# Two self-attentions of a decoder: second scores nine heads behind, weighted products a quarter later, turned maxima in the last quarter of a step

## The reference, cut to what matters

```python
att = jnp.einsum('bhqd,bhkd->bhqk', q, k) * (1.0 / np.sqrt(HD))
att = jnp.where(causal[None, None], att, -jnp.inf)   # the first only
att = jax.nn.softmax(att, axis=-1)
y = jnp.einsum('bhqk,bhkd->bhqd', att, v)
```

## Time and profile before

| what | us |
|---|---|
| median of 3 runs (lowest, highest) | 941.11 (940.72, 942.71) |
| the profiled execution | 941.59 |
| its span, first to last instruction | 939.7 |
| PE busy | 847.7 (90% of the span) |
| DVE busy | 561.1 (60%) |
| ACT busy | 480.4 (51%) |
| POOL busy | 256.1 (27%) |

### The profile page before, as it was taken

How to read it: one execution, slowest core, us unless ns; L and a number is a source line. 1 busy time by engine, 2 the same in 40 slices (tenths; PEclk the granted TensorE clock), 3 DMA queues, 4 the chain that set the end, 5 groups by cost and what they waited for, 6 DMA issues and landing times.

```text
span 939.7 us, 19518 instructions
## 1 busy us (share of the span) xinstructions
PE 847.7 (90%) x6498; PEld 695.7 (74%) x6498; DVE 561.1 (60%) x1561; ACT 480.4 (51%) x1154; POOL 256.1 (27%) x541
## 2 busy tenths in 40 slices
PE   5999879999999999999999968885897888887788
PEld 3888668888888888888888756663796566665565
DVE  3876466555655566655655347774544577666474
ACT  2455465555555555555555315664464476677141
POOL 3864120000000000000000047551075577776110
PEclk9999999999999999999999989999899899999995
DMA  7000000000000000000000030001222000000000
GB/s 270 2 2 1 1 1 1 1 1 1 0 0 0 0 0 0 0 0 0 0 0 0 1 115 1 2 1 28 88 47 59 1 1 0 0 0 0 24 1 22
DMA packets 9410, 15.85 MB, mean 17 GB/s; under 512 B 816, under 2 KB 5040, under 8 KB 8976
## 3 DMA queue, kind: packets, MB, share of 16 engines
q1 hardware_dynamic: 8400, 13.23, 4.2%
q0 software_dynamic: 960, 1.97, 0.9%
HBM read 13.16 MB, written 2.03 MB: 16 GB/s over the span
## 4 chain that ended last, share of the span: by engine, by line
PE 76%; ACT 7%; DVE 6%; issue 6%; POOL 3%; DMA 1%; ACTq 1%; DVEq 0%; POOLq 0%; SPq 0%
PE psum L875 9%; PE psum L887 9%; PE psum L855 5%; PE psum L856 5%; PE psum L857 5%; PE psum L847 5%; PE psum L598 4%; ACT arena L1301 4%; PE psum L840 3%; PE psum L617 3%; PE psum L635 3%; PE psum L956 2%; PE psum L566 1%; PE psum L1034 1%; PE psum L648 1%
## 5 line engine op out<-in xcount | busy, mean ns | idle before, releaser
L1818 DVE TENSOR_REDUCE xnegmax<-psum 128x1 f32<-128x768 f32 x128 | 122.4, 956 | 139.5 <-PE psum L857 139.3
L1405 ACT ACTIVATE arena<-psum,xnegmax 128x768 f32<-128x768 f32 x128 | 115.5, 903 | 139.5 <-DVE xnegmax L1818 97.8
L2265 POOL COPY acur<-A_all 128x128 f32 (+1 forms) x18 | 5.2, 293 | 388.1 <-PE psum L840 388.1
L875 PE MATMUL psum<-pack_a,arena 128*128 128x128 f32 x768 | 106.8, 275 | 0.2 <-ACT arena L1396 0.2
L1249 ACT ACTIVATE arena<-psum 128x384 f32<-128x384 f32 (+1 forms) x128 | 69.5, 546 | 71.2 <-PE psum L620 42.1
L855 PE MATMUL psum<-kv_high,xq_high 128*128 128x384 f32 x256 | 101.5, 396 | 1.8 <-DVE kv_low L1813 1.6
L875 PEld LDWEIGHTS psum<-pack_a,arena 128*128 128x128 f32 x768 | 87.5, 141 | 13.9 <-issue 12.3
L1396 ACT ACTIVATE arena<-psum 128x512 f32<-128x512 f32 x128 | 75.9, 593 | 42.5 <-PE psum L875 42.5
L887 PE MATMUL psum<-arena,xv 128*64 128x256 f32 x768 | 89.9, 383 | 0.0
L856 PE MATMUL psum<-kv_low,xq_high 128*128 128x384 f32 x256 | 86.8, 339 | 0.0
L857 PE MATMUL psum<-kv_high,xq_low 128*128 128x384 f32 x256 | 86.7, 339 | 0.0
(11 more groups left out here) (309 smaller groups left out, 1853.6 us busy)
## 6 DMA issues: line engine op xcount, KB each, us to landing
w1all<-in_w SPq DMA_DIRECT2D x1, 2048.0 KB, 8.2
arena<-in_w SPq DMA_DIRECT2D x1, 2048.0 KB, 10.8
pack_v<-in_pack_v SPq DMA_DIRECT2D x1, 1088.0 KB, 9.0
pack_l<-in_pack_l SPq DMA_DIRECT2D x1, 1079.5 KB, 12.0
pack_q<-in_pack_q SPq DMA_DIRECT2D x1, 1024.0 KB, 6.9
pack_a<-in_pack_a SPq DMA_DIRECT2D x1, 653.0 KB, 6.1
pack_f<-in_pack_f SPq DMA_DIRECT2D x1, 556.0 KB, 9.9
x<-in_x SPq DMA_DIRECT2D x2, 256.0 KB, 3.0
```

The lines of the kernel that those rows point to most:

```text
L875: last = transpose(bank[4 + (3 * u + c) % 2][:, (2 * i + h) * P:(2 * i + h + 1) * P], xprob[:, u % 2, h * KEYS + kt * P:h * KEYS + (kt + 1 ...
L1405: activation(xprob[:, u % 2, half * KEYS:(half + 1) * KEYS].rearrange("p (c w) -> p c w", c=2), src, ACT.Exp, bias=xnegmax[:, u % 2, half: ...
L1818: v.tensor_reduce(xnegmax[:, u % 2, half:half + 1], banks_pair(half), AX.XY, ALU.max, negate=True)\
```

## The change

One constant and a few conditions of the three order loops change. Nothing is computed that was not computed before.

```diff
-LAG = 8
+LAG = 9
@@ PE
-                        if j == 0 and 0 <= it - 3 < H:
+                        if j == 1 and 0 <= it - 3 < H:
                             weighted(it - 3)
-                        if j == 1 and it >= 7 and (it - 7) % G == 0:
+                        if j == 2 and it >= 7 and (it - 7) % G == 0:
                             result_turned((it - 7) // G)
-                        if j == 2 and 0 <= it - 1 < H:
+                        if j == 3 and 0 <= it - 1 < H:
                             maxima_turned(it - 1)
-                        if j == 2 and 0 <= it - 3 < H:
+                        if j == 3 and 0 <= it - 3 < H:
...
                             back_to_tokens(it - 3)
@@ ACT
-                        if j == 1 and 0 <= it - 3 < H:
+                        if j == 2 and 0 <= it - 3 < H:
                             empty_weighted(it - 3)
-                        if j == 1 and it >= 7 and (it - 7) % G == 0:
+                        if j == 2 and it >= 7 and (it - 7) % G == 0:
                             result_ready((it - 7) // G)
@@ DVE
-                for it in range(H + 3):
+                for it in range(H + 4):
...
-                        if j == 2 and 0 <= it - 1 < H:
-                            shifted_queries(it - 1)
-                        if j == 3 and 0 <= it - 3 < H:
-                            divided(it - 3)
+                        if j == 0 and 0 <= it - 2 < H:
+                            shifted_queries(it - 2)
+                        if j == 0 and 0 <= it - 4 < H:
+                            divided(it - 4)
                     aside(it)
```

## The result

The changed kernel takes 966.25 us (median of 4 runs, 965.66 to 967.72) where the kernel before takes 941.63 in the same runs: a ratio of 1.0263 [1.0245, 1.0281]. It is slower by 24.6 us. The forecast was slower by 18.2; the time lies 0.25 us above the upper end of the range. The profiled execution took 966.82 us with a span of 965.0, against 941.59 and 939.7.

A forecast was written before the change was run, and what follows sets the result against it. Both loops were taken to run at the pace of PE's stream. Att1's intervals 10.0, att0's 4.8 and norm work 3.4 sum to 18.2 us, giving 959.3 from the median of 941.11; range 951 to 966.

The forecast's parts named there:

- Head and end: First and last steps of each attention: one first scores more ahead, one less at the end; 0, within 1 us each.
- The interval in att1: Turned maxima to weighted products in att1: each interval 0.77 us longer, waiting for shifted queries; 13 intervals, 10.0 us.
- rival 3: More idle time on PE lowers the granted clock for 2 us in each of 13 att1 steps: 972 us, chance 0.03.
- rival 1: In att1 the new wait takes the place of the turned maxima's old 0.53 wait: 952.4 us, chance 0.08.
- rival 2: POOL's split holds att1's turned maxima; the extra quarter frees them, saving up to 7.1 us: 934.0, chance 0.03.
- rival 4: No difference: the turned maxima's wait goes and the new wait takes back as much: 941 us, chance 0.02.
- ACT's copy of slots: It also waits for the shifted queries, but PE reads its keys only in the next step: taken at nothing.
- the weights are not pulled ahead: At the shifted queries' reader, the load starts after the wait; pulled ahead, it would save 3.9 us, giving 955.4.
- the 2.75: Summed length in us of att1's new interval from turned maxima to weighted products, against 1.98 before.
- att0's intervals: Turned maxima to weighted products in att0: 3.08 against 2.71 us, 0.37 longer in 13 intervals, 4.8 us.
- the norm work: DVE work ending att0 steps 2, 4, 6, 8 delays the next maxima by 0.96 or 0.74, two each: 3.4 us.

The follow-up runs named there:

- the sixth experiment: Kernel before, with turned maxima and back to tokens moved past three score pairs and shifted queries directly behind, weighted products unmoved: 935.05 us, ratio 0.9893.
- the fifth experiment: Kernel before, with only the shifted queries on DVE moved a quarter later, behind one further head's maxima: 955.4 us, ratio 1.0126.
- the first experiment: Changed kernel, with the shifted queries put directly behind the step's last maxima on DVE, ahead of norm work and next maxima: 945.64 us, ratio 1.0008 to before.
- third experiment: Changed kernel, with norm work of att0 steps 2, 4, 6, 8 put behind the shifted queries and two maxima: 964.61 us, ratio 1.0214 to before.

## Why the prediction came out below the time

The mechanism was forecast rightly; the sum was too small, 18.2 us for 24.6. Three of its steps failed. Head and end, put at 0, measured 1.8 us. The interval in att1, put at 0.77, measured 0.85 to 0.93, which is 1.4 us in all. And the clock, for which the sum had no term because rival 3 was put away, fell behind the longest wait of att0, 1.35 us. Without any one of the three the time would have come out inside the range, whose end it passed by 0.25.

**Right: the mechanism and its place.** In every full interval of att1 L617 waits for L1620, W to M is as long as before (2.73 against 2.72) and L648 still waits 0.53. With that rivals 1, 2 and 4 are out: the new wait ate nothing of the old one, and M does not go earlier. The changed kernel gave POOL's split of the maxima the extra quarter of rival 2, and the wait stayed; the sixth experiment put a third score pair between W and M, and it went. So the copy sets M. The term put at nothing, ACT's copy of slots, was rightly so: in att1 L1240 waits for Q 13 times, 7.1 us, but PE stands still for keys only once, 0.4.

**Right: the weights are not pulled ahead.** The load of the reader's weights in the step above:

```profile
622.10 0.31 PEld L598 LDWEIGHTS psum<-kz,slots 128*128 128x128 f32 x2
623.25 0.30 PEld L617 LDWEIGHTS psum<-qs,kz 128*128 128x128 f32 x2 [0.84 <-DVE qs L1620]
```

It starts 0.05 after Q's end (622.79 + 0.41 = 623.20) and not during the 0.84 us in which the loader was idle. The Trainium skill, page "TensorE: Matmul & The Clock Gate", section "Step-by-step: what each phase is for", has loads pulled ahead of matmuls in flight. For this load the row decides against it. The weights here are the keys of a head, which the first scores have read nine heads earlier; the late queries are the other operand. So it is the wait ahead of the load that held it.

**Mis-sized: the interval in att1, 0.77.** Of the thirteen intervals, forecast at 10.0 us, twelve grew by 0.85 to 0.93 and the last by 0.62, 11.4 together. Two terms of the 2.75 were too short. The slots took 621.74 - 621.19 = 0.55 and not 0.48; from the reader to W it was 623.69 - 623.26 = 0.43 and not 0.33. Both prices came from rows with other neighbours ahead. From the reader to W it is 0.43 behind a wait, of 0.64 here and of 0.17 in the fifth experiment, and 0.33 in the sixth without one. The slots are not a matter of the wait: they take 0.56 behind back to tokens in the sixth experiment too (609.47 to 610.03), where M does not wait. The sum left out the slow start of the row behind M, 0.09 in the old order, which now falls on the slots.

**Right in size: att0's intervals and the norm work.** The plain intervals grew by 0.38 (forecast 0.37), 5.0 in 13. The norm work gave 3.6 beyond that (forecast 3.4), though not evenly: the first step 1.76 in all instead of 1.33, half of it since DVE came to the moments 0.20 later than thought and half since this interval was 2.46 and not 2.71 before; the others 1.01, 1.30 and 1.01 for 1.11, 1.33 and 1.11.

**Wrong: "head and end, I take 0".** In att0 the first scores come 0.43 earlier against the first M (in the first experiment too, so this is M's place), and the first M to the second takes 4.49 instead of 3.67 (3.68 in the first experiment, so this too is Q's place); with -0.2 at the end that is +1.0. In att1 the way to the second M gives 0.5 and the last two intervals -0.23 + 0.53 = 0.3. Head and end are 1.8 us in place of 0, inside the bounds of 1 us for each attention, but both on the same side. The reason given for group 0, that DVE is behind there anyway, was one for a longer wait, not for none.

**Wrong: the clock.** Rival 3 was priced as a fall in each step of att1 and put away. It came as single falls. The first stands in att0. Busy time and granted clock in stretches of 2 us (columns as in the earlier trace rows), kernel after:

```profile
34.00:36.00 2.00, 0.67 (x7) 0.49 (x6) 1.97 (x14) 0.49 (x1) 0.88 (x3) 1.00 0.00 0
36.00:38.00 2.00, 1.80 (x24) 1.23 (x25) 0.68 (x3) 1.09 (x2) 1.04 (x2) 0.99 0.00 0
38.00:40.00 2.00, 2.00 (x12) 1.72 (x12) 0.71 (x3) 0.77 (x2) 1.92 (x5) 0.50 0.00 0
40.00:42.00 2.00, 2.00 (x15) 2.00 (x14) 0.53 (x2) 0.49 (x1) 1.89 (x4) 0.66 0.00 0
```

Behind the stretch with the 1.53 us wait, in which PE was busy for 0.67 of 2.00, the clock went to 0.50, the lower level (1.2 GHz), for some 3 us. W to M took 3.69 there instead of 2.75, and the next M to W 3.51 instead of 3.10: 1.35 us. In the second profile of the kernel the same two took 4.05 and 4.29, which is 2.5 us. None of the other eight profiles has a fall between the first scores and the last W of either attention. With the norm work moved behind (third experiment) the same place shows no long wait and no fall:

```profile
34.00:36.00 2.00, 1.82 (x21) 1.40 (x24) 1.90 (x8) 1.30 (x3) 1.25 (x4) 1.00 0.00 0
...
38.00:40.00 2.00, 1.97 (x19) 1.78 (x18) 1.04 (x5) 0.83 (x3) 1.83 (x5) 1.00 0.00 0
```

The Trainium skill, the same page, section "What's actually happening", has the clock halved for a TensorE that is not kept busy. The trace agrees here in so far as a stretch with 0.67 of 2.00 stands some 2 us ahead of the 0.50.

A second fall stands at the end of att1, where eight matmuls (L673) close the attention; first the kernel after, then the first experiment:

```profile
673.72 2.07 PE L673 MATMUL psum<-pack_f,arena 128*128 128x128 f32 x8 [0.47 <-ACT arena L1262]
```

```profile
653.53 1.16 PE L673 MATMUL psum<-pack_f,arena 128*128 128x128 f32 x8 [0.47 <-ACT arena L1262]
```

From the last start of L659 to the end of this row it is 1.04 us longer than in the first experiment. Both profiles of after have it (2.07 and 2.08), and so has the kernel with the norm work moved (2.08). But it does not hang on Q's place: with Q right behind M the sixth experiment shows 1.92, and the second profile of the kernel before 1.39. At the end of att0 the same eight matmuls take 1.82 us in one profile of after and 1.16 in the other, and up to 2.08 in experiments. So the 1.04 us are counted below as clock, but that they come from the change is not shown. In the 16 us ahead of this row PE's rows start at the same distances in after and in the first experiment, to 0.05 us.

**The account.** In the profiled pair the span grew by 25.3 where 18.2 was forecast, 7.1 more. The intervals of att1 have 1.4 of it, its head and end 0.8, att0's head and end 1.0, its intervals and the norm work together 0.4, the clock there 1.35, and the clock at the end of att1 1.04. That leaves 1.1 us for stages which the change does not touch, among them the 1.5 that the second profiles do not repeat and the start's -0.8; their cause was not sought further.

## What to carry to other kernels

When a producer's place is moved on one engine, ask what its new neighbour ahead has to wait for: here Q stood behind maxima that wait for scores on PE, and a short way turned into PE - DVE - PE with nothing beside it. The price of such a wait is the way over the other engine less the work left beside it, taken from rows that have the same neighbours ahead, and the head of the loop has to be priced too (0.8 us between the first two turned maxima of att0). Where a line waits for a copy, move that line alone past more work and keep its successors directly behind it: that took 1.1% off in the median of four runs, and moving the copy's own source along with it left the wait as it was.

## What the hardware showed beyond that

- One wait of 1.53 us in a loop that PE otherwise fills was followed by a granted clock of 0.50 although PE was busy in the 2 us after it for 1.80 and then for 2.00, and so in the second profile (1.54 us); a wait of 1.01 us at the same place (norm work alone ahead of Q, one profile) was not. The fall cost about as much as the wait itself, 1.35 us in one profile, and more, 2.5, in the other.
- The spacing of PE's rows depends on what stands ahead of them: from second scores to W 0.43 behind a wait against 0.33 without one, and the slots 0.55 or 0.56 behind the transposes of M and back to tokens, with or without a wait, against 0.48 behind second scores. In a step of att1 this made 2.89 us out of the summed 2.75.
